# Second expert layer routed in two parts, batch 0 first in the conditioning, odd identities behind the copies

## The reference

```
x = x + attn0(cond(x, f, f, w0, u0, c));   x = x + ffn0(cond(x, f, f, w1, u1, c))
x = x + attn1(cond(x, f, f, w2, u2, c));   x = x + ffn1(cond(x, f, f, w3, u3, c))

cond(r, k, v, w, u, c):        # tf = sigmoid(sum(c)); decay = exp(-exp(w)) * (0.5 + 0.5 * tf)
    ek, ekv = exp(min(k, 30)), exp(min(k, 30)) * v
    nf, df = forward scans of ekv, ek: a = a * decay + in;   nb, db = the same in reverse
    euk = exp(min(u + k, 30))
    num, den = nf + nb - ekv + euk * v, df + db - ek + euk
    return sigmoid(r) * (num / max(den, 1e-8)) * (0.8 + 0.2 * tf)

attn0: 16 heads of 16; logits and probabilities are each mixed over heads by low-rank terms
       and by per-token diagonals that are computed from the tokens
attn1: 32 query and 8 key heads of 8, rotary positions, causal softmax
ffn0:  16 experts, top 4, gated, and a shared expert
ffn1:  gate = softmax(x @ Wg + bg) over 8 experts, top 2;
       h = gelu(gelu(x @ W1 + b1) @ W2 + b2); out = sum over the two of gate * (h @ W3 + b3)
```

## Time and profile before

| what | value |
|---|---|
| median of three executions | 1203.2 us (1197.13 to 1207.09) |
| the profiled execution | 1195.22 us, span 1192.4 us |
| busy: TensorE, VectorE, ScalarE, GpSimd | 83%, 66%, 50%, 18% of the span |
| mean granted TensorE clock | 0.94 of full |
| chain that ended last, by engine | TensorE 42%, VectorE 22%, DMA 14%, ScalarE 13% |
| SyncE's issue of wu, xT, causal (the last of attention's loads) | 1.20, 2.14, 7.17 us |
| first matmul | 32.02 us |
| last outputs of the second attention turned | 939.90 us |
| first transposes of the second expert layer's tiles | 997.90 us |

### The profile page before, as it was taken

The page is one execution under the profiler, slowest core; times in us unless marked ns, Lnnn a source line. Parts: engine busy times, 40 slices in busy tenths (PEclk is TensorE's granted clock), DMA queues, the critical chain, the costliest instruction groups (busy, mean ns, idle before and its releaser), DMA issues.

```text
span 1192.4 us, 18413 instructions
## 1 busy us (share of the span) xinstructions
PE 993.7 (83%) x6320; PEld 707.5 (59%) x6320; DVE 790.8 (66%) x2033; ACT 599.5 (50%) x1452; POOL 213.1 (18%) x179
## 2 busy tenths in 40 slices
PE   0789888988898889779988889789889676999995
PEld 0667676767676667554655666433333355887884
DVE  4568987887789778864488884666767341554542
ACT  3279727863886288431533332256657612544442
POOL 1000020102010201117333333000000031222323
PEclk9989999999999999979999999789989956999998
DMA  9999500000000000034588885135545336586772
GB/s 269 247 226 242 114 1 1 2 1 1 1 2 1 1 1 1 1 110 164 171 279 271 283 281 187 47 142 212 187 166 212 142 131 228 171 238 205 228 218 27
DMA packets 74876, 161.28 MB, mean 135 GB/s; under 512 B 10642, under 2 KB 56990, under 8 KB 70432
## 3 DMA queue, kind: packets, MB, share of 16 engines
q1 hardware_dynamic: 65904, 145.52, 39.9%
q0 software_dynamic: 8880, 14.60, 4.8%
HBM read 127.68 MB, written 62.62 MB: 160 GB/s over the span
## 4 chain that ended last, share of the span: by engine, by line
PE 42%; DVE 22%; DMA 14%; ACT 13%; issue 5%; POOL 2%; SPq 1%; ACTq 0%; POOLq 0%; DVEq 0%
PE ps L1520 39%; DMA out<-arena 8%; ACT arena L606 3%; DMA arena<-in_w0all 3%; DMA made<-arena 2%; DVE arena L1047 2%; DVE arena L1023 2%; DVE arena L1353 2%; ACT arena L584 2%; ACT arena L591 2%; POOL out L507 2%; DVE den L904 1%; DVE arena L985 1%; ACT arena L599 1%; ACT arena L577 1%
## 5 line engine op out<-in xcount | busy, mean ns | idle before, releaser
L1520 PE MATMUL ps<-arena 128*128 128x256 f16 (+15 forms) x4712 | 780.6, 341 | 78.8 <-ACT arena L599 29.3
L1520 PEld LDWEIGHTS ps<-arena 128*128 128x128 f32 (+8 forms) x4712 | 531.3, 149 | 254.2 <-issue 105.5
L1504 DVE CAST arena<-arena 128x256 f16<-128x256 f32 x120 | 36.5, 304 | 111.7 <-ACT arena L794 111.7
L1353 DVE TENSOR_REDUCE arena<-ps 128x4 f16<-128x1024 f32 (+1 forms) x48 | 58.8, 1227 | 50.4 <-PE ps L1520 50.4
L448 POOL TENSOR_TENSOR den<-den,backd 128x512 f32<-128x512 f32 x9 | 11.4, 1268 | 424.2 <-DVE euv L892 424.2
L794 ACT ACTIVATE arena<-ps,arena 128x256 f32<-128x256 f32 x120 | 56.0, 475 | 59.7 <-PE ps L1520 57.6
L1047 DVE SCALAR_TENSOR_TENSOR arena<-arena 128x128 f32<-128x128 f32 x240 | 83.7, 409 | 0.5
L606 ACT ACTIVATE arena<-ident,arena 128x128 f32<-128x128 f32 x256 | 80.9, 388 | 0.0
L1014 DVE SCALAR_TENSOR_TENSOR arena<-arena,ps 128x128 f32<-128x128 f32 (+1 forms) x128 | 47.4, 411 | 48.1 <-PE ps L1520 41.8
L507 POOL DMA_INDIRECT out<-arena x30 | 47.1, 1570 | 147.2 <-DMA out<-arena 87.0
L477 POOL DMA_INDIRECT made<-arena x47 | 53.1, 1129 | 101.2 <-DVE arena L1266 100.2
(11 more groups left out here) (281 smaller groups left out, 1286.9 us busy)
## 6 DMA issues: line engine op xcount, KB each, us to landing
arena<-split SPq DMA_DIRECT2D x15, 2048.0 KB, 9.1
arena<-in_w0all SPq DMA_DIRECT2D x47, 608.0 KB, 5.0
slots<-in_blank SPq DMA_DIRECT2D x17, 1040.0 KB, 16.4
arena<-in_w1all SPq DMA_DIRECT2D x16, 1024.0 KB, 6.6
split<-arena SPq DMA_DIRECT2D x32, 512.0 KB, 3.7
slots<-in_blank SPq DMA_DIRECT2D x9, 1072.0 KB, 18.4
arena<-slots SPq DMA_DIRECT2D x47, 130.0 KB, 3.4
arena<-slots SPq DMA_DIRECT2D x15, 268.0 KB, 2.9
```

The source lines that it names most:

```text
L1353: dve.tensor_reduce(out, ps[:, at:at + 2].rearrange("p j (r s) -> p j r s", r=nr), X, ALU.max, negate=True).then_inc(max1_done, 1)
L1520: return pe.matmul(o, l, r, start=start, stop=stop, skip_group_check=shared)
```

## The change

Three things are edited.

First, the start. kT is loaded in two pieces, batch 0 (own semaphore, "first") and the rest (counted with xT and the identity). The first two small loads are no longer waited for together with kT. VectorE bounds only batch 0, ScalarE takes the exponential of batch 0 alone, and the rest follows: its bound (rest_bounded) between the first scans, its exponential on ScalarE behind the first slice's, its product behind condition_batch(0, 0, 1). In slice 0 GpSimd only adds backn and euv to num; den is summed on VectorE (first_sums), and only finish waits for GpSimd. Unused zerob and zero32 go.

Second, in attention 0, diagonals_post of an odd head moves behind the next pair's turn_out calls. Even heads stay.

Third, the routing of the second expert layer is in two parts, HEAD = 6 tiles (batches 0 to 2) and the last two. Its tensors move from the arena to the space of kT, ek and ekv (side), and the combined weights are written into rows_out directly. The head's sigmoid stands on ScalarE ahead of the last maxed_out, its product on VectorE in the last half's first step, its 24 matmuls on TensorE ahead of the last half's last values; softmax, choice, rows, sums, ranks and places of the head stand between normalising, turning and projecting the last outputs. The last two tiles follow. GpSimd scatters the twelve DMAs of the head when their ids are there, then the last four. SyncE loads the first two tiles' rows ahead of the base's store.

```diff
+HEAD = TAU - TT
...
+        side = sb("side", 3 * CT * NT)
+        kT, ek, ekv = (side[:, n * CT * NT:(n + 1) * CT * NT].rearrange("p (c t) -> p c t", c=CT) for n in range(3))
...
-            load(kT[:], d["fT"], ld["cond"])
+            load(kT[:, :, 0:T], d["fT"][:, :, 0:T], ld["first"])
+            load(kT[:, :, T:], d["fT"][:, :, T:], ld["x"])
...
-            sp.wait_ge(base_ready, 4)
-            sp.dma_start(out[0:NT].rearrange("(a p) c -> p a c", p=P), base).then_inc(base_out, 16)
             sp.wait_ge(scattered, 16 * 2 * TAU)
             tile_rows(0)
             tile_rows(1)
+            sp.wait_ge(base_ready, 4)
+            sp.dma_start(out[0:NT].rearrange("(a p) c -> p a c", p=P), base).then_inc(base_out, 16)
...
-            sum_slice(0)
+            pool.wait_ge(sums_in, 1)
+            st(pool.tensor_tensor(num[:], num[:], backn[:], ALU.add))
+            st.settle()
+            st.tell(pool.tensor_tensor(num[:], num[:], euv[:], ALU.add), sums_out, 1)
...
+            for stage, taus in enumerate((range(HEAD), range(HEAD, TAU))):
+                pool.wait_ge(slots_ready, stage + 1)
+                for tau in taus:
+                    for k in range(2):
+                        pool.indirect_dma_start(slots[:], bass.IndirectOffsetOnAxis(ap=slot_ids[:, k, tau:tau + 1], axis=0),
+                                                rows_out[:, tau], None).then_inc(scattered, 16)
...
-            act.wait_ge(c_dve, 5)
-            act.activation(ek[:], ek[:], ACT.Exp).then_inc(c_act, 1)
+            act.wait_ge(c_dve, 2)
+            act.activation(ek[:, :, 0:T], ek[:, :, 0:T], ACT.Exp).then_inc(c_act, 1)
             exp_slice(0)
+            act.wait_ge(c_dve, 7)
+            act.activation(ek[:, :, T:], ek[:, :, T:], ACT.Exp).then_inc(c_act, 1)
...
                         turn_out(2 * p - 2)
                         turn_out(2 * p - 1)
+                        diagonals_post(2 * p - 1)
...
                             normalise(n)
-                            diagonals_post(n)
+                            if n % 2 == 0:
+                                diagonals_post(n)
...
+                if i + 2 == 2 * B:
+                    sigmoid_rows(slice(0, HEAD * P), B - 1)
                 if i + 1 < 2 * B:
                     maxed_out(i + 1)
                 outputs_out(i)
...
+            exp_rows(slice(0, HEAD), 3)
+            high_rows(0)
             o1T_out(B - 1)
+            high_rows(1)
+            high_rows(2)
+            sigmoid_rows(slice(HEAD * P, NT), B)
+            exp_rows(slice(HEAD, TAU), 4)
+            high_rows(3)
...
+                if first:
+                    return [lambda: forward(num, ekv), rest_bounded, lambda: backward(backn, ekv), own_term, lambda: forward(den, ek),
+                            lambda: backward(backd, ek), first_sums, floor, *(lambda q=q: invert(q) for q in range(4)), finish]
...
+                    if k == 0 and i + 1 == 2 * B:
+                        condition_rows(3, slice(0, HEAD * P), 4, 2)
...
+            first, last = slice(0, HEAD), slice(HEAD, TAU)
+            logits1(first, 2, 3)
+            normalise(2 * B - 1)
+            shares(pr1[:, first], mx1[:, first], 5)
+            choose1(first)
+            low_rows(0)
+            residual1(B - 1)
+            sum_tiles(first, 1)
+            condition_rows(3, slice(HEAD * P, NT), 6, 3)
+            combine(first, 1)
+            low_rows(1)
+            low_rows(2)
+            place_rows(first, 3, 1)
+            logits1(last, 4, 4)
+            shares(pr1[:, last], mx1[:, last], 7)
+            choose1(last)
+            sum_tiles(last, 2)
+            combine(last, 2)
+            dve.wait_ge(route_pe, 5)
             count = ps[:, 1, TAU * E1:(TAU + 1) * E1]
...
                     table_ready, 1)
+            low_rows(3)
+            place_rows(last, 5, 2)
...
+                else:
+                    pe.wait_ge(ld["moe1"], 7 * 16)
+                    route(wg1, E1, 2, range(HEAD))
                 values(i, 5)
...
+            turn_outputs(2 * B - 1)
+            turn_rows(0)
+            turn_o(B - 1)
+            turn_rows(1)
+            project_out(B - 1)
+            turn_rows(2)
+            ranks1(slice(0, HEAD), 1)
+            route(wg1, E1, 3, range(HEAD, TAU))
+            turn_rows(3)
+            ranks1(slice(HEAD, TAU), 2)
+            pe.wait_ge(comb_ready, 2)
```

More of the change, by code:

```diff
@@ L892, in own_term, with first_sums @@
                     st.tell(dve.tensor_tensor(euv[:], euk[:], kT[:, :, cols], ALU.mult), sums_in, nth + 1)
+                def first_sums():
+                    dve.wait_ge(*done["scan"])
+                    st(dve.tensor_tensor(den[:], den[:], backd[:], ALU.add))
+                    st.settle()
+                    st(dve.tensor_tensor(den[:], den[:], euk[:], ALU.add))
+                    st.settle()
                 def floor():
-                    if not early:
+                    if not early and not first:
                         dve.wait_ge(sums_out, nth + 1)
@@ L1446, in _, with combine, low_rows @@
+            def combine(part, told):
+                n = part.stop - part.start
+                for k in range(2):
+                    st(dve.tensor_tensor(placed[:, k, part], oh1[:, k, part], spread(top1[:, part, k], 2, E1), ALU.mult))
+                st.settle()
+                st.tell(dve.tensor_tensor(rows_out[:, part, C:C + E1], placed[:, 0, part], placed[:, 1, part], ALU.add),
+                        comb_ready, told)
+            def low_rows(q):
                 dve.wait_ge(high_ready, q + 1)
@@ new lines, in place_rows @@
+            def place_rows(part, done, told):
+                n = part.stop - part.start
+                dve.wait_ge(route_pe, done)
+                ranks = ps[:, 1, part.start * E1:part.stop * E1].rearrange("p (a e) -> p a e", e=E1)
+                st(dve.tensor_tensor(place[:, part], ranks, spread(iota_rows, 1, n), ALU.add))
+                dve.wait_ge(comb_ready, told)
+                st.settle()
+                for k in range(2):
+                    st(dve.tensor_tensor(placed[:, k, part], oh1[:, k, part], place[:, part], ALU.mult))
+                st.settle()
+                for k in range(2):
+                    st(dve.tensor_reduce(slotf[:, k, part], placed[:, k, part], X, ALU.add))
+                st.settle()
+                st.tell(dve.tensor_copy(slot_ids[:, :, part], slotf[:, :, part]), slots_ready, told)
@@ L1999, in _, with turn_rows @@
                     turn_stacks(b + 1, 0)
[L2000 to L2007 removed]
+            def turn_rows(q):
                 for half in range(2):
```

209 lines of the change are left out of this document (100 added, 109 removed).

## The result

The changed kernel took 1182.7 us (median of 4 runs, 1179.79 to 1189.69), the kernel before 1204.3 us beside it (4 runs, 1197.13 to 1207.09): a ratio of 0.985, 95% interval 0.9807 to 0.9892. The forecast was 1183.0, 20.2 us less. The profiled execution of after is 1180.62 us long (span 1178.8).

A forecast was written before the change was run, and what follows sets the result against it. The prediction saw an unoverlapped start, attention pairs and engine handovers before the second expert layer as bounds. Gains 7.5 + 2.8 + 9.9 = 20.2 us took the 1203.2 us median to 1183.0 us, range 1173 to 1195 (own range 1175 to 1190).

The forecast's parts named there:

- Part 1: At the start, conditioning batch 0 first lets TensorE start at 24.5 instead of 32.02: gain 7.5 us, bounds 4 to 10.
- the wait for the identity: At the start, VectorE's minimum over the other three batches waits 0.2 us for xT and the identity, landed about 9.6.
- The contention with GpSimd: At the start, GpSimd's two remaining sums slow VectorE's scans of den by 2.1 us, bounds 0 and 2.5.
- Rival (b): Start held by loads: if xT and the identity land at 14, gain there is 3.5, total 1187.0 us; chance 0.08.
- Part 2: In layer 0's attention, moving odd identities behind the copies gains 0.7 us a batch, 2.8 over four; bounds -1 and 5.
- the cost at a batch's end: In layer 0's attention, where no scores follow, VectorE waits for the later odd exponential: 0.4 us lost a batch.
- Rival (c): Identities delay every attention pair's chain: a pair loses 1.0, 28 pairs lose 28 us, total 1213.8 us; chance 0.06.
- Part 3: Between second attention and second expert layer, two-part routing brings the first expert tile earlier: gain 9.9 us, bounds 3 to 12.
- T comes 4.8 later: At the seam, T (second attention's last outputs turned) is delayed by ScalarE's added 3.0 and TensorE's routing 1.9 us.
- The head's route: Six tiles' routing, 24 matmuls on TensorE ahead of the last values, costs 1.9 us there, bounds 0 and 2.6.
- the term of 10.0 from the last scatter to the first tile: At the seam, the first expert tile follows the last scatter's start by 10.0 us, as in the kernel before.
- Rival (a): Seam gives only part, as engine handovers add waits: base sums start at T'+30, gain 4, total 1188.9 us; chance 0.20.

The follow-up runs named there:

- e12: Changed kernel with tanh for sigmoid, head's route after the last values, tile 1's weights after first rows, GpSimd's start sums later: 1175.88 us, ratio 0.9792 to before.
- e1: The changed kernel again, unedited, on another chip than the first measurement: 1177.88 us, ratio 0.9895 to the kernel before.
- e2: The kernel before with only the new start (batch 0 first): 1184.0 us, ratio 0.9936 to the kernel before.
- e3: The changed kernel with the two-part routing undone, so new start and moved odd identities only: 1184.74 us, ratio 0.9943 to the kernel before.
- e9: The changed kernel a third time, unedited, on a further chip: 1188.08 us, ratio 0.9896 to the kernel before.
- e11: Changed kernel with tile 1's weights after the first rows and 42 unused matmuls in TensorE's waits before the base sums: 1182.26 us, ratio 0.9849 to before.
- e4: The kernel before with only the odd heads' identities moved: 1190.33 us, ratio 1.0004 to the kernel before.
- e10: The changed kernel with the odd identities back at their old place: 1187.6 us, ratio 0.9898 to the kernel before.
- e6: Changed kernel with thirteen unused matmuls filling TensorE's wait while ScalarE loads tables ahead of the last outputs: 1182.58 us, ratio 0.9843 to before.
- e7: Changed kernel with the head's 24 routing matmuls behind the last half's last values instead of ahead: 1182.04 us, ratio 0.9838 to before.
- e8: Changed kernel with the weights of tile 1 issued behind the first two tiles' rows instead of ahead: 1188.04 us, ratio 0.9884 to before.
- the two longer comparisons: The unedited changed kernel against the kernel before, on two other chips with more runs: ratios 0.9895 and 0.9896.
- e5: Changed kernel with the routing gate as tanh, in the exponential's table, instead of sigmoid: 1185.14 us, ratio 0.9861 to before.

## Why the prediction was right, and where its steps were not

The time came out within the range, but the closeness of the number is luck. All three parts gave less than forecast, and the first comparison gave more than the three together.

**Part 1, forecast 7.5.** The mechanism came as worked out, and 7.4 in the first profile. Over eleven profiles with part 1 (all but e12) the first matmul is at 24.6 to 26.7, mostly 26.0: a gain of 6.0, and ten of them miss the forecast's 24 to 25. The term that was too small is the wait for the identity in front of the minimum over the other batches: 0.2 in the forecast (landed at 9.6), 0.51 in after, and 1.8 to 2.4 in the ten other profiles, where it landed at 11.7 to 12.5; by the forecast's own sign a wait over 1 us is a step that's wrong. The first profile was the exception, not the rule. Part of the delay is the change's own doing: the 9.6 is xT's landing in before (issued at 2.14), while the identity was issued at 2.62 and landed 7.4 later, at 10.0; with kT's load in two pieces SyncE issues it only at 3.68, which makes 11.1 with the same 7.4. The rest is that its landing takes 6.7 us in after and 7.9 to 8.7 in e1, e2, e3, e9 and e11. The contention with GpSimd, 2.1 in the forecast from a nearby row, was 2.0, and e12 shows it as a cost that moving two sums takes away. The rule of the Trainium skill that was weighed there (SBUF — State Buffer, "SBUF: two separate sides") fits in kind, as both engines read two operands; by the whole length of each sum it would be, as an estimate, 2.5 to 3.0 (sums of 1.26 alone, 1.48 and 1.52 here), and 2.0 was measured. Rival (b), the front held by its loads, is in this sense partly true, at 1.5 us rather than 4.

**Part 2, forecast 2.8.** The attention of batch 0 is 2.1 us shorter (mean 102.9 in the eleven profiles with part 2, 105.0 in the three without), and the stretch from the first matmul to the last pair of batch 3 is 2.5 shorter (451.2 against 453.7 us, the same profiles). So it isn't 0.7 in each of four batches: batches 1 to 3 make 0.4 of it together, and even that comes from a single long gap in before's profile. The step that failed is the cost at a batch's end. The forecast had 0.4 for VectorE's longer wait there; it is 0.6 (1.08 instead of 0.46), and TensorE then waits 0.8 us longer for VectorE's last mix (1.49 instead of 0.71 us), which gives back what the first pair won. That the gain reaches the program's end, which the forecast took for granted, is not borne out either: e4 and e10 show no difference. Rival (c), the slower case, is excluded: the steady pairs are 8.78 apart.

**Part 3, forecast 9.9.** It gave 6.3 in the profiles (76.1 to 69.8 from R to the first tile) and 6.9 in the totals of e3 and e1. The step "T comes 4.8 later" failed: it came 7.6 later. ScalarE's 3.0 was right (2.97). The head's route was put at 1.9; and the step that took all of TensorE's work there at full clock left out that the engine which waits for a late exponential also loses its clock, 1.6 us by e6. The other 1.2 of the difference I put down to the route at a size of 3.1 rather than 1.9. In after's trace its 24 matmuls take 2.8 us of TensorE's time at full clock, so the 1.9, which hid a part of them in a wait, was too small; that e7, which moves only the route, wins 1.2 fits this but doesn't prove it. Behind T the forecast of 43.3 was measured as 44.4 to 45.1. There the term of 10.0 from the last scatter to the first tile, taken from before, was too small for the rows, 11.7 in after: the weights of tile 1 now lie in the queues beside the scatters, which e8 shows. The 10.0 was also another wait. In before SyncE has the base ahead of the rows, and asks for the rows 5.0 us behind the last scatter because the base is stored only then:

```profile
991.83 0.40 SPq L424 DMA_DIRECT2D out<-arena  x1
992.98 4.33 SPq L313 DMA_DIRECT2D arena<-slots  x3
```

The base, forecast as the later one, is in fact 0.6 to 1.4 us ahead of the rows. Rival (a), a seam that gives only part, has its direction here, though not its place: the base did start at T+24 to T+25.

**The sum.** By the profiles' typical sizes the parts make 6.0, 0 to 2.5 and 6.3, together 12 to 15 us, which is what the two longer comparisons found (12.4 and 14.4). The forecast of 20.2 met the first comparison's 21.6 because that one lay well above what the parts make; why it did isn't shown (four runs of each kernel, some 10 us from lowest to highest). That the kernel is faster was right on each chip. That it is by over 1% is sure only in the first comparison; the other two ratios, 0.9895 and 0.9896, lie just beyond that limit, and their intervals reach across it.

## What to carry to other kernels

When work is hoisted into an engine's stream ahead of a handover, price not only the delay but what the waiting engine loses: here 3 us of table loads and a gate cost TensorE another 1.6 us through its granted clock, and a function that stands in the table already loaded gave back 3.2. When work is moved behind a handover, look at the end of the loop too, where nothing follows that would hide it. Compare small edits by the stretch between two milestones that they enclose, and not by totals: here the stretches repeated within about a microsecond where the totals moved by 10 from chip to chip. Where two inputs of one step arrive within a microsecond, as the rows and the base here, speed up both or neither.

## What the hardware showed that was not expected

- The granted clock of the base sums fell to 0.50 in e11 while TensorE was busy without a break, 2.6 us into them, though it had stood at 1.00 since 950. In after it was 0.50 for all of their 18.5 us, with TensorE as busy. In this case's rows a busy TensorE didn't get its clock back for these small f32 matmuls. In e5 the clock also fell to 0.50 within the head's route (matmuls of 8 columns), in e6 right behind it, each after 4 to 5 us of work without a break. The Trainium skill (TensorE: Matmul & The Clock Gate, Part 1) lets sustained activity release the clock; for these sums that was not seen.
- The exponential's and the gate's table change in 1.28 us with no drain behind the load, at the seam as at the start: 915.07 + 1.28 = 916.35, and the gate starts at 916.37.
- A wait of up to 12.4 us (2.84 without the pause) of three engines at one place of the program, which appears on some chips or at some times and not on others, and that no releaser explains. The matmuls behind it are 1.5 to 4.5 us slower.
